# The second layer's expert rows get a dispatch buffer of their own, filled with zeros beforehand

## The reference

```python
x = x + L0_ffn(L0_cond(x, cond_512))      # modulated projection, then 8 gated experts (88 x 2 hidden) + a shared one
x = x + L1_ffn(L1_cond(x, cond_512))      # low-rank adapter; attention (16 heads of 8), then 8 experts (512 hidden)

# in each ffn
logits = h @ gate;  topv, topi = top_k(logits, 2);  w = softmax(topv)
y      = sum over the two chosen experts e of  w_e * expert_e(h)
```

## Time and profile before

| | us |
|---|---|
| median of 3 runs | 783.62 |
| lowest, highest | 779.27, 787.50 |
| the profiled execution | 779.83 |
| its span | 778.0 |
| PE busy | 614.0 (79%) |
| DVE busy | 479.8 (62%) |
| POOL busy | 431.9 (56%) |
| ACT busy | 383.5 (49%) |

### The profile page before, as it was taken

The page is one execution under the profiler, slowest core; times in us unless marked ns, Lnnn a source line. Parts: engine busy times, 40 slices in busy tenths (PEclk is TensorE's granted clock), DMA queues, the critical chain, the costliest instruction groups (busy, mean ns, idle before and its releaser), DMA issues.

```text
span 778.0 us, 17752 instructions
## 1 busy us (share of the span) xinstructions
PE 614.0 (79%) x5541; PEld 486.0 (62%) x5541; DVE 479.8 (62%) x1522; ACT 383.5 (49%) x838; POOL 431.9 (56%) x571
## 2 busy tenths in 40 slices
PE   5878882987778828884999999999972299999892
PEld 2446461877768816552676666666651199999892
DVE  3535352645455566754787787778645178886666
ACT  3333310444344415865767777777642155665441
POOL 2755651365545665552555678777757135664453
PEclk9989987899999965988899999999995599999997
DMA  7911114655566640855243434343401798887657
GB/s 237 217 38 38 47 39 118 178 163 145 151 164 182 198 175 1 252 168 202 58 106 85 123 98 122 105 116 109 101 29 48 188 284 256 234 260 247 205 199 239
DMA packets 91833, 115.24 MB, mean 148 GB/s; under 512 B 16144, under 2 KB 69424, under 8 KB 91632
## 3 DMA queue, kind: packets, MB, share of 16 engines
q1 hardware_dynamic: 76768, 92.63, 42.2%
q0 software_dynamic: 9088, 18.76, 7.0%
q10 hardware_dynamic: 5904, 2.94, 1.4%
HBM read 80.75 MB, written 33.53 MB: 147 GB/s over the span
## 4 chain that ended last, share of the span: by engine, by line
PE 29%; issue 8%; DVE 6%; POOL 5%; another core or an unknown queue 2%; DMA 1%; ACTq 1%; ACT 1%; DVEq 0%; POOLq 0%; SPq 0%
PE psO L2008 7%; PE psA L912 6%; PE ps L1840 3%; PE psAO L1870 2%; PE psAO L1879 2%; POOL dispatch_rows L356 2%; PE ps L1852 2%; PE ps L1850 2%; DVE mneg L1694 1%; PE psT L862 1%; DMA dispatch_rows<-tail 1%; POOL rstd L1446 1%; PE psW L1889 1%; DVE X L2046 1%
## 5 line engine op out<-in xcount | busy, mean ns | idle before, releaser
L356 POOL DMA_INDIRECT dispatch_rows<-row,index x128 | 126.6, 989 | 74.1 <-DVE index L337 41.7
L921 POOL DMA_INDIRECT expert_rows<-eo,to x78 | 82.7, 1060 | 80.9 <-ACT eo L1067 59.3
L921 POOL DMA_INDIRECT expert_rows<-fo,to x78 | 81.3, 1042 | 80.4 <-DVE fo L2019 56.3
L1694 DVE TENSOR_REDUCE mneg<-ps 128x4 f32<-128x512 f32 x128 | 86.2, 676 | 45.8 <-PE ps L1840 36.6
L1790 ACT ACTIVATE arena<-ps 128x512 f32<-128x512 f32 x128 | 75.6, 591 | 56.0 <-PE ps L1852 55.3
L894 DVE CAST xh<-psT 128x256 fp32r<-128x256 f32 x78 | 32.8, 421 | 88.2 <-PE psT L862 54.2
L912 PE MATMUL psA<-xh,wh 128*128 128x256 f32 (+1 forms) x234 | 74.2, 317 | 13.5 <-DVE xl L898 13.4
L1840 PE MATMUL ps<-km,qp 96*128 96x512 f32 x128 | 63.5, 503 | 10.3 <-ACT km L1783 7.3
L1783 ACT ACTIVATE km<-kp,const 96x512 fp32r<-96x512 f32 x96 | 67.9, 714 | 5.9 <-PEq L1152 4.6
L912 PE MATMUL psA<-xh,wl 128*128 128x256 f32 (+1 forms) x234 | 67.5, 289 | 0.0
L912 PE MATMUL psA<-xl,wh 128*128 128x256 f32 (+1 forms) x234 | 67.4, 288 | 0.0
(11 more groups left out here) (226 smaller groups left out, 1552.8 us busy)
## 6 DMA issues: line engine op xcount, KB each, us to landing
wb<-in_W1b SPq DMA_DIRECT2D x29, 578.0 KB
w<-in_W SPq DMA_DIRECT2D x29, 304.0 KB
qk_parts<-qk SPq DMA_DIRECT2D x8, 1024.0 KB, 4.2
qp<-qk_parts SPq DMA_DIRECT2D x48, 128.0 KB
kp<-qk_parts SPq DMA_DIRECT2D x48, 128.0 KB
qm<-qk_parts SPq DMA_DIRECT2D x192, 32.0 KB
arena<-in_W1b SPq DMA_DIRECT2D x10, 578.0 KB
V<-expert_rows SPq DMA_DIRECT2D x8, 512.0 KB
```

The costliest lines, as they stand in the source:

```text
L356: pool.indirect_dma_start(out=m.xbuf, out_offset=bass.IndirectOffsetOnAxis(ap=r.index[b][:, c:c + 1], axis=0), in_=r.row[b][:, c // TOPK, ...
L921: pool.indirect_dma_start(out=m.ybuf, out_offset=bass.IndirectOffsetOnAxis(ap=to[b][:, a:a + 1], axis=0), in_=out[b][:, a, :], in_offset=N ...
L1694: nc.vector.tensor_reduce(mneg[s % 2][:, g, :], ps1[:, g % 2, :].rearrange("p (j k) -> p j k", j=4), AX_X, ALU.max, negate=True).then_inc( ...
```

## The change

The second layer gets a second buffer, `late_rows`, of the same size. All rows of its eight regions that a tile can reach (4096 each) are filled with the zero row, and so are its dead tiles, before the first scatter to it. Layer 1 then needs no tails. The fills are issued by SP: the dead tiles and the regions 0 to 5 in `layer0`, behind the later loads and `table_sync`; the regions 6 and 7 in `attention`, behind the masked queries of pairs 2 and 3. A region is two DMAs of 1.06 MB, in pieces of 1040 bytes. POOL waits for all seventeen at the start of lap 10.

`lead_loads` is split in two, `lead_weights` and `lead_rows`; layer 0 now calls `table_fill` ahead of `lead_weights`, so the tails no longer wait for `tabled` 1 and the weights stand behind them.

Two more things move in `pre_attention`: the zeroing of `m.qm` goes from DVE to POOL, and the loads are spread over the groups. Group 2 issues pair 0 and a quarter of the masked queries of pair 0, group 3 pair 1 and another quarter, groups 4 and 5 a quarter each, groups 6 and 7 half of those of pair 1 each.

```diff
+    m.xbufs = [nc.dram_tensor(name, (E * REGION + E * SLOTS, ROW), F32, kind="Internal").ap()
+               for name in ("dispatch_rows", "late_rows")]
+    m.filled = m.sem("filled")
...
+FILLS = 2
+EARLY_FILLS = 6
+def fill_region(m, sp, e):
+    tiles = TOK // SLOTS // FILLS
+    rows = m.tail[:, e].rearrange("p a c -> p (a c)").unsqueeze(1).to_broadcast([P, tiles, 2 * ROW])
+    for f in range(FILLS):
+        at = e * REGION + f * tiles * SLOTS
+        sp.dma_start(m.xbufs[1][at:at + tiles * SLOTS].rearrange("(i p a) c -> p i (a c)", p=P, a=2), rows
+                     ).then_inc(m.filled, 16)
+def fill_dead(m, sp):
+    sp.dma_start(m.xbufs[1][E * REGION:].rearrange("(e a p) c -> p e a c", a=2, p=P), m.tail[:, E:]).then_inc(m.filled, 16)
...
@@ layer0, SP
                 table_sync(tiles, sp)
-                lead_loads(m, sp, tiles, [...], d["W123"], [...], [...], range(E))
+                fill_dead(m, sp)
+                for e in range(EARLY_FILLS):
+                    fill_region(m, sp, e)
+                table_fill(tiles, sp, range(E))
+                lead_weights(m, sp, tiles, d["W123"], [w[:] for w in m.lead_w])
+                lead_rows(m, sp, tiles, 16 * (E + 1), [...], m.xbufs[0], [x[:] for x in m.lead_xs])
...
@@ pre_attention, SP
+MASKED_EARLY = {2: (0,), 3: (1,), 4: (2,), 5: (3,), 6: (4, 5), 7: (6, 7)}
                     if n == 2:
                         sp.wait_ge(qk_out[0], 16)
-                        for pair in range(2):
-                            load_pair(m, sp, pair, pair)
-                    if n in (3, 4):
                         sp.wait_ge(m.zeroed, 2)
-                        load_masked(m, sp, n - 3)
+                    if n in (2, 3):
+                        load_pair(m, sp, n - 2, n - 2)
+                    for part in MASKED_EARLY.get(n, ()):
+                        load_masked(m, sp, part // 4, (part % 4,))
...
@@ pre_attention, POOL (and the same two lines removed from DVE)
+                for b in range(2):
+                    nc.gpsimd.memset(m.qm[b][:].bitcast(F32), 0.0).then_inc(m.zeroed, 1)
                 pool.wait_ge(cleared, 2)
+                pool.wait_ge(m.zeroed, 2)
...
@@ attention, SP
-                table_sync(tiles, sp)
+                    if k in (2, 3):
+                        fill_region(m, sp, EARLY_FILLS + k - 2)
                 sp.wait_ge(mixed, SEQS)
-                lead_loads(m, sp, tiles, [...], d["W1b"], m.late_w, m.late_xs, range(TAIL_ACT, E))
+                lead_weights(m, sp, tiles, d["W1b"], m.late_w)
+                lead_rows(m, sp, tiles, 16 * (FILLS * E + 1), [...], m.xbufs[1], m.late_xs)
@@ attention, POOL
                 for s in range(LAPS):
+                    if s == 10:
+                        pool.wait_ge(m.filled, 16 * (FILLS * E + 1))
@@ attention, ACT
-                table_fill(tiles, act, range(TAIL_ACT))
```

More of the change, by code:

```diff
@@ L356, in route_scatter @@
         pool.indirect_dma_start(
-            out=m.xbuf, out_offset=bass.IndirectOffsetOnAxis(ap=r.index[b][:, c:c + 1], axis=0),
+            out=r.xbuf, out_offset=bass.IndirectOffsetOnAxis(ap=r.index[b][:, c:c + 1], axis=0),
             in_=r.row[b][:, c // TOPK, c % TOPK, :], in_offset=None).then_inc(r.scattered[b], 16)
@@ L375, in __init__ @@
         self.is_e, self.val, self.val2 = (sb(x, [P, ETILES, E1]) for x in ("is_e", "val", "val2"))
-        self.link, self.ended, self.tabled, self.tails = m.sems(*(s + tag for s in (
-            "tt_link", "ended", "tabled", "tails")))
+        self.link, self.ended, self.tabled = m.sems(*(s + tag for s in ("tt_link", "ended", "tabled")))
+        self.tails = m.sem("tails0") if tag == "0" else m.filled
 def table_fill(w, engine, experts):
@@ L386, in table_fill @@
                                min_val=e * REGION, max_val=e * REGION + TOK)
-        engine.dma_start(m.xbuf[bass.ds(at, SLOTS), :].rearrange("(a p) c -> p a c", p=P), m.tail[:, e]
+        engine.dma_start(m.xbufs[0][bass.ds(at, SLOTS), :].rearrange("(a p) c -> p a c", p=P), m.tail[:, e]
                          ).then_inc(w.tails, 16)
@@ L808, in lead_buffers, with lead_weights @@
     m.lead_xs = [m.sb(f"lead_xs{b}", [P, 2, ROW], ctx=ctx) for b in range(LEAD)]
-def lead_loads(m, sp, tiles, scattered, weights, w, xs, fills):
+def lead_weights(m, sp, tiles, weights, w):
     sp.wait_ge(tiles.tabled, 1)
@@ L816, in lead_loads, with lead_rows @@
         sp.dma_start(w[b], weights[bass.ds(e, 1)].rearrange("e p h -> (e p) h")).then_inc(m.ld[b], 16)
-    table_fill(tiles, sp, fills)
+def lead_rows(m, sp, tiles, tails, scattered, xbuf, xs):
     sp.wait_ge(tiles.tabled, 2)
@@ L1221, in lows @@
                             in1=qk[b][:, 2 * w, :].bitcast(F32), op0=ALU.add, op1=ALU.subtract).then_inc(low, 1)
-                for b in range(2):
-                    nc.vector.memset(m.qm[b][:].bitcast(F32), 0.0).then_inc(m.zeroed, 1)
                 for h in range(HALVES):
@@ L1556, in attention_loads, with load_masked @@
     m.zeroed = m.sem("a_zeroed")
-def load_masked(m, sp, k):
-    for j in range(4):
+def load_masked(m, sp, k, heads=range(4)):
+    for j in heads:
         for r, a in enumerate((0, 1, 0)):
```

24 lines of the change are left out of this document (11 added, 13 removed).

## The result

The changed kernel takes 769.02 us (median of 4 runs, 767.32 to 771.82); the kernel before, run beside it, 782.32 us (779.27 to 787.50). The ratio is 0.985 with an interval of 0.980 to 0.989: faster, though by less than 2%, and by 13 us in the medians. The forecast was 771 us. The profiled execution took 771.82 us, against 779.83 before, and the two spans differ by 9.0 us.

A forecast was written before the change was run, and what follows sets the result against it. No engine bounds the kernel throughout; TensorE stands still at hand-overs between five blocks. Terms -5.0 - 5.0 + 1.0 - 1.2 - 3.5 + 0.4 + 1.5 = -11.8 us gave 771 us, own range 765 to 776, wider range 763 to 782.

The forecast's parts named there:

- F: Attention to experts 1: without tails the first rows are issued earlier, -5.0 us, bounds -4.0 to -5.8.
- A: Layer 0 to experts 0: tails go ahead of the weights, so rows are issued earlier, -5.0 us, bounds -3.5 to -5.7.
- H: Layer 0: 13.8 MB of fills on SP's queue may cause a general slowdown, +1.0 us.
- Rival 1: Layer 0 pays under the fills, +15 us instead of +1, total about 786 us; chance 0.13.
- B: Before attention: zeroing `qm` on POOL frees VectorE for its first addition, -1.2 us, bounds 0 to -1.9.
- C: Before attention: spread pair and mask loads shorten the stall for `gbu` of group 6, -3.5 us, bounds 0 to -5.6.
- D: Before attention: six mask issues stand between the last two stores, +0.4 us, bounds 0 to 1.
- E: Attention: loads of pairs 4 and 5 come late behind fills of regions 6 and 7, +1.5 us, bounds 0 and +6.3.
- the sign of being wrong: Attention: the prediction would be wrong if laps 5 to 8 stretch by more than 4 us together.
- Rival 2: Attention: pair loads queue behind the fills, +6.3 us instead of +1.5, total 776.6 us; chance 0.14.
- Rival 4: Only the hand-overs pay, the spread loads before attention giving nothing: -8.3 us, total 775 us; chance 0.12.
- Rival 3: Layer 0: fills not over at 114 us (below 177 GB/s) hold tails, weights and rows; some 805 us; chance 0.07.

The follow-up runs named there:

- the buffer alone: Changed kernel with weights ahead of tails in layer 0, zeroing on VectorE and loads bunched, as before the change: 780.24 us, ratio 0.988.
- the first group: Runs of four changed-kernel variants (weights ahead of tails, eight regions early, bunched loads, half regions): 707.4, 717.66, 710.47, 707.5 us; kernel before 706.15 us.
- third experiment: Changed kernel with pair and masked loads before attention in their old bunches, zeroing still on POOL: 710.47 us, ratio 1.006.
- the two moved regions: Changed kernel with two of layer 0's six region fills moved to the start of the block before attention: 770.97 us, ratio 0.986.
- the two with moved regions: Two changed-kernel variants filling two regions at the start of the block before attention, taken from layer 0 (770.97 us) or from attention (768.59 us).
- eight regions: Changed kernel with regions 6 and 7 also filled in layer 0, none in attention: 717.66 us, ratio 1.017.

## Why the prediction held, step by step

**F, hand-over behind attention, forecast -5.0: right.** Measured -5.3 in the first pair of traces, -6.1 between the kernel before and the buffer alone. The rows follow the last scatter by 1.65 us; the forecast had taken 1.9 from the barrier behind experts 0. What was under-sized is the cost before: 6.95 us is the lowest of four traces that reach to 8.85.

**A, hand-over out of layer 0, forecast -5.0: right in sign and place, 0.5 to 1 us too large.** Measured -4.05 (-4.5 between the changed kernel and the buffer alone). Two sizes were off, by +3.5 and -1.3 us. The eight tails now run beside the last eight scatters, which end at 122.60, and take 12.01 us; I had used 8.53 us from a stretch in which the scatters were over. That the scatters are the reason fits all traces outside the first group, but no run tests it by itself. The weights take 1.52 instead of 2.85. So they are out at 129.08 instead of 126.4. Beside them ACT stood until 121.31 for a "remote" release and VectorE until 123.45, so that `tabled` 2 came at 128.52 instead of 123.2 before; SP's own work ends at the same time, so this stall cost little, but it would hold the rows if the tails were quicker.

**H, fills in layer 0, forecast +1.0: right.** +0.9 in the first pair, and 122.1 to 124.4 in all traces with fills against 120.6 to 124.1 without: the means differ by 1.5 us, inside the spread. Rival 1 falls: most waits ahead of the groups stay near 3 us while the queues carry 296 GB/s. A single wait of 6.1 us, near 48, turns up without fills and in two traces with them, and in the others not at all, so the fills do not make it. What they may make is one longer wait: between 60 and 90 one wait of 3.8 to 4.8 us stands in five of the six traces with fills, where the four of the kernel before reach 3.2. That is the size of the term, and it is a reading, not a test.

**B, zeroing on POOL, forecast -1.2: right.** The first addition of VectorE comes 1.46 us earlier, in every trace. In the first pair only 0.39 of it is left at group 1, at group 2 it is -1.68; the marks of group 2 vary by 0.75 us in the kernel before alone, so what it is worth further on is known to about 1 us only.

**C and D, spread loads, forecast -3.1 together: -1.9 in the traced pair, -3.0 in the first group; C about right, D under-sized.** From `x2` of group 5 to that of group 7 the changed kernel needs 14.54 us instead of 17.86: -3.3 for C, forecast -3.5. Over the five traces with either layout outside the first group the means are 14.5 and 17.3: -2.8. D was put at +0.4, bounds 0 to 1; it is +1.45, outside the bounds. From `x2` of group 7 to attention it is 15.64 us instead of 14.19. Below, TensorE's last products and the window over them in the changed kernel; then TensorE and SP in its second trace.

```profile
343.19 1.92 PE L1377 MATMUL psV<-wqkv,hT 128*128 128x128 f32 x8
344.90 2.63 PE L1371 MATMUL psQK<-hT,wqkv 128*128 128x512 f32 x4
```

```profile
341.66:345.66 4.00, 3.06 (x13) 2.63 (x14) 0.75 (x1) 2.76 (x6) 0.00 (x0) 0.67 0.49 141
```

```profile
344.39 1.06 PE L1377 MATMUL psV<-wqkv,hT 128*128 128x128 f32 x8
345.42 1.98 PE L1371 MATMUL psQK<-hT,wqkv 128*128 128x512 f32 x4
...
345.70 3.36 SPq L1595 DMA_DIRECT2D qm<-qk_parts  x6
349.16 0.38 SPq L1191 DMA_DIRECT2D qk_parts<-qk  x1
354.97 1.25 SPq L1129 DMA_DIRECT2D qp<-qk_parts  x3
```

In the first trace the granted clock falls (mean 0.67 of the window, the lower level of 1.2 GHz for part of it) behind an idle time of 2.29 us, and `psV` takes 1.92 instead of 1.06. In the second trace it stays full behind the same idle time (2.30), and the last store, behind six mask loads, takes 5.2 us to land instead of 4.0. Both come to 15.65 us. Over all eight traces with spread loads it is the same: 15.62, 15.63 and 15.66 us in the three with a full clock and a late store, 15.64 to 15.85 in the five with a fallen clock and a store that lands in 4.0 to 4.2. With the loads bunched and the clock full (third experiment and the kernel before) the stretch is 14.19 us; bunched with a fallen clock (the buffer alone) it is 15.83. So the masks between the stores cost 1.45 us where the clock is full, and a fallen clock costs about as much where they are not in the way. In no trace do the two add. The step of mine that failed is D's size: I counted six issues (0.4 us), not that the last store, issued behind them, lands later. Why the clock falls in some traces and not in others, at the same idle time, isn't settled.

**E, fills in attention, forecast +1.5: right, though the first pair shows +3.9.** Up to the first scatter, that is up to lap 10, where the fills can act, the traces with fills need 0.9 to 2.0 us more than the 73.6 of the kernel before (mean 1.4), and without fills it is 73.8. In the first pair this part is +2.0. It lies where the forecast put it, at the pair loads behind the fills: from the mark of lap 6 to that of lap 9, 19.69 us instead of 17.92, +1.8. In this stretch lies POOL's second wait for keys (3.96), and ACT's (1.71). The first wait (2.16) lengthens no lap. Laps 5 to 8 together stretch by 1.8 us; 4 was to be the sign of being wrong. The other +1.9 lies between the first and the last scatter, where four traces of the kernel before differ by 1.9 themselves. The means, 171.9 and 172.9, leave room for 1 us that I didn't foresee and can't tell from chance. The fills in attention are not its cause: in the first group this stretch is 160.97 to 161.03 us in all four traces, with fills in attention and without. Rival 2 had the mechanism that E has too, a pair load late behind a region; its price of 6.3 us falls. POOL's two waits for keys sum to 6.1 us, but the first was slack, and the stretch up to the first scatter grows by no more than 2.0.

The Trainium skill (DMA: Bandwidth & Descriptors, Queues, rings and completion order) says that on one engine descriptors of a ring are consumed in order. The traces agree: a pair load behind a whole region comes late (POOL waits 4.0 us, behind a half region not at all), and in the first group the rows come 10.8 us later when two more regions stand ahead of them.

**Experts 0 and 1, forecast nothing: -2.85 and +1.95.** Nothing in these traces ties them to the change. Near the end of experts 0 one scatter of POOL takes 5.5 to 7.7 us in some traces and 1 in others. Timeline of the kernel before, then of the changed kernel:

```profile
276.02 6.72 POOL L921 DMA_INDIRECT expert_rows<-eo,to  x1 [0.31 <-issue]
```

```profile
275.37 0.96 POOL L948 DMA_INDIRECT expert_rows<-eo,to  x1 [0.31 <-issue]
```

It is there in three of four traces of the kernel before and in two of six with the own buffer (the zeroing on VectorE, 7.72, and the two moved regions, 7.72), so the own buffer does not rule it out. Experts 0 takes 153.4 to 158.1 us with it and 150.5 to 153.3 without. The first pair of traces happened to have it before and not after. Experts 1 varies between 162.6 and 173.2 in the kernel before alone.

**Rival 4** (only the hand-overs pay) falls by the bunched loads: 3.0 us. **Rival 3** did not happen at 770 us. At 706 us its mechanism did, and the point I gave for it, 13.8 MB in 78 us, was in effect a statement on the length of layer 0, which I had taken as fixed. The rate was no worry (some 250 GB/s for the fills alone, where 177 decide); the cover was.

So the sum, -11.8, came out as -9.0 in the traced pair and -13.3 in the medians, through terms that were each within 1.5 us except E in this one pair. A fairer count takes the means of four traces of the kernel before and of four with tails first, spread loads and zeroing on POOL (the changed kernel twice and the two with moved regions). The stretches with a term then differ by +1.6 (H), -4.3 (A), -3.4 (B, C, D), +2.0 (E) and -6.2 (F), together -10.3. The two blocks of experts, without a term, add -3.6, which is why the medians came so near the forecast: the mechanisms gave 1.5 us less than I said, and that the time did not show it is luck. These two stretches vary by more than most terms.

## What to carry to other kernels

Zeros written early to save tails late are free only as long as the stretch that covers them is longer than they are; everything else on the same issuing queue stands behind them. The end of their issue is not the end of their transfer (80.6 and about 91 us here), so read the DMA share, and leave a margin for a shorter stretch (here layer 0 took 104 us in one group of runs and 123 in the others), or put part of them where the DMA engines idle (here the start of the block before attention, share 0.05). Where a load stands behind a fill on the queue, a smaller piece can make it free: 1.06 MB ahead of a pair cost no lap (one trace), 2.13 MB cost 0.8 to 1.8 us. A total that doesn't move is no proof that a change did nothing: look at the laps. Sum a forecast over marks, and take each mark from several traces before calling a difference of 2 us an effect.

## What the runs showed of the hardware

- The kernel before took 703.6 to 711.7 us in one group of runs and 777.5 to 791.8 us in others (no trace of it fell in the first). In the traces of the variants waits for "remote" releases sum to 0.0 us in the four of the first group and to 100 to 172 us in the ten others, while scatters last the same (980 and 984 ns).
- The eight tails took SP 8.5 to 9.2 us to issue in the kernel before, and 11.2 to 12.5 us beside indirect scatters of POOL (five traces with the tails first, outside the first group; 8.9 in the sixth, with the old order).
- With fills of 1040-byte pieces beside scatters the queues moved 296 GB/s, at a DMA share of 1.11, against 43 GB/s in the same stretch without them; with no engine busy, fills and the first tails moved 321 GB/s (window 104 to 116 with eight regions).
- Twelve fills of 1.06 MB are issued some 10 us before the last of them has moved (issued until 80.6, share 1.00 until 90).
- Behind the same idle time of 2.3 us the granted clock fell in six of fourteen traces and stayed full in eight.
- One of POOL's indirect scatters can take 5.5 to 7.7 us instead of 0.96: a single one in five of the ten traces outside the first group, none in the four of it, always near the end of experts 0.
